# Attention rotation on GpSimd: eight 128x512 operations a step regrouped into four 128x1024 operations, with the minus sign moved into a VectorE product

## The reference

```python
def _apply_rope(x):
    ...
    x1, x2 = jnp.split(x, 2, axis=-1)
    rot = jnp.concatenate([-x2, x1], axis=-1)
    return x * cos + rot * sin
...
q = _apply_rope(proj(Wq, bq))        # 16 heads of 64
k = _apply_rope(proj(Wk, bk))
v = proj(Wv, bv)
scores = jnp.einsum('bhnqd,bhnkd->bhnqk', qb, kcat) * scale   # blocks of 128 queries, 256 keys
attn = jax.nn.softmax(jnp.where(valid, scores, -1e30), axis=-1)
ctx = jnp.einsum('bhnqk,bhnkd->bhnqd', attn, vcat)
return merged @ Wo.T + bo
```

## Time and profile before

| what | value |
|---|---|
| median of three runs | 1629.46 us (1627.92 to 1631.04) |
| span of the profiled execution, first to last instruction | 1627.8 us |
| own time of the profiled execution | not listed apart from the three runs |
| mean granted TensorE clock | 0.983 |
| VectorE busy from 300 to 1400 us | 999.38 us |
| TensorE busy from 300 to 1400 us | 1044.70 us |
| ScalarE busy from 300 to 1400 us | 905.92 us |
| GpSimd busy from 300 to 1400 us | 772.60 us |

### The profile page before, as it was taken

How to read it: one execution, slowest core, us unless ns; L and a number is a source line. 1 busy time by engine, 2 the same in 40 slices (tenths; PEclk the granted TensorE clock), 3 DMA queues, 4 the chain that set the end, 5 groups by cost and what they waited for, 6 DMA issues and landing times. The chain is left out here.

```text
span 1627.8 us, 46635 instructions
## 1 busy us (share of the span) xinstructions
PE 1505.6 (92%) x16930; PEld 1152.3 (71%) x16930; DVE 1401.5 (86%) x3881; ACT 1318.2 (81%) x2394; POOL 1031.1 (63%) x788
## 2 busy tenths in 40 slices
PE   5999978899999999999999999999999999869998
PEld 4888745576766777676767666766777677658887
DVE  5999678899999899999998998999899989857885
ACT  5999657888878888878887887878888878849996
POOL 4665267677667777767677776667777767513443
PEclk8999999999999999999999999999999999979999
DMA  5233246989998989899998999998989899962331
GB/s 210 91 124 107 78 85 120 175 152 191 157 184 162 179 157 181 168 176 176 163 179 157 179 164 175 157 182 163 175 162 182 154 174 154 176 159 69 109 106 75
DMA packets 721530, 247.90 MB, mean 152 GB/s; under 512 B 687380, under 2 KB 706072, under 8 KB 721304
## 3 DMA queue, kind: packets, MB, share of 16 engines
q1 hardware_dynamic: 720600, 244.53, 77.4%
q10 hardware_dynamic: 704, 0.40, 0.1%
HBM read 47.73 MB, written 25.17 MB: 45 GB/s over the span
## 5 line engine op out<-in xcount | busy, mean ns | idle before, releaser
L1450 ACT ACTIVATE at_prob<-at_prob,at_top 128x256 f32<-128x256 f32 (+1 forms) x1024 | 428.5, 490 | 42.1 <-DVE at_top L1262 39.0
L1262 DVE CUSTOM_DVE_ANT_0 at_prob<-banks,at_masks,pre_s_scale 128x256 f32<-128x256 f32 (+1 forms) x1024 | 420.3, 471 | 19.7 <-PE banks L1703 6.7
L1585 PE MATMUL banks<-at_xt,pre_w_h 128*128 128x512 f16 x1024 | 297.5, 383 | 22.6 <-ACT at_v_l L1478 21.9
L1274 DVE TENSOR_TENSOR at_halves<-at_prob,at_halves 128x1024 f16<-128x1024 f32 (+1 forms) x256 | 315.5, 1233 | 1.2 <-ACT at_halves L1459 1.2
L1703 PE MATMUL banks<-at_kt,at_qt 32*128 32x256 f32 (+1 forms) x4096 | 251.6, 382 | 38.8 <-POOL at_qt L1183 19.5
L1459 ACT ACTIVATE at_halves<-at_prob 128x1024 f16<-128x1024 f32 (+1 forms) x256 | 263.4, 1029 | 6.1
L1703 PEld LDWEIGHTS banks<-at_kt,at_qt 32*128 32x128 f32 x4096 | 197.4, 186 | 99.8 <-issue 95.5
L1204 POOL TENSOR_TENSOR at_c_halves<-at_ctx,at_c_halves 128x1024 f16<-128x1024 f32 x64 | 136.7, 2136 | 178.0 <-DVE at_halves L1274 172.4
L1173 POOL TENSOR_TENSOR at_kt<-at_k_by 128x512 f32<-128x512 f32 x128 | 163.2, 1275 | 95.6 <-DVE at_halves L1274 95.4
L1183 POOL TENSOR_TENSOR at_qt<-at_q_by 128x512 f32<-128x512 f32 x128 | 223.0, 1761 | 0.0
L1163 POOL TENSOR_TENSOR at_q_by<-at_q_first,at_tables 128x512 f32<-128x512 f32 x128 | 163.2, 1275 | 83.5 <-DVE at_halves L1274 83.5
(11 more groups left out here) (128 smaller groups left out, 3280.4 us busy)
## 6 DMA issues: line engine op xcount, KB each, us to landing
f_x<-in_x SPq DMA_DIRECT2D x16, 512.0 KB, 3.7
x_after_ffn<-f_x SPq DMA_DIRECT2D x16, 512.0 KB, 2.6
at_x_ln<-x_after_ffn SPq DMA_DIRECT2D x16, 512.0 KB, 3.5
at_x_res<-x_after_ffn SPq DMA_DIRECT2D x64, 128.0 KB, 3.0
x_after_attention<-at_x_res SPq DMA_DIRECT2D x64, 128.0 KB, 2.7
f_x<-x_after_attention SPq DMA_DIRECT2D x16, 512.0 KB, 4.6
out_x<-f_x SPq DMA_DIRECT2D x16, 512.0 KB, 3.0
at_tables<-in_cos SPq DMA_DIRECT2D x16, 256.0 KB, 4.0
```

What stands on the lines that cost most here:

```text
L1262: last = nc.vector.tensor_tensor_reduce(out=prob[:, n % 2, h, low:2 * P], in0=s_ps[:, h, n % 2 * 2 * P + low:(n % 2 + 1) * 2 * P], in1=mas ...
L1274: nc.vector.tensor_tensor(parts[:, 1, :, :], prob[:, n % 2, :, keys_from(t, b):2 * P], parts[:, 0, :, :], ALU.subtract).then_inc(p_low, 1)
L1450: last = nc.scalar.activation(at, at, ACT.Exp, bias=top[:, n % 2, h:h + 1], scale=-1.0)
L1585: last = nc.tensor.matmul(pr_ps[:, half, :].rearrange("p (b t) -> p b t", b=SB), w[wp][:, k, at:at + P], xt[:, r, xp, :, k, :], start=n == ...
```

## The change

The rotation is regrouped. On GpSimd the two products of a first half (with cos and with sin) become one operation of 128x1024, and so do the two halves of the sum. For this the difference becomes a sum: VectorE writes the sin product of the second half with its sign turned, as (-bias - x) sin, with a table of negated biases made once. Each step then has four GpSimd rotation operations where there were eight, and as many VectorE products as before. The semaphores of single products are merged: a consumer that waited for one half waits for both.

The order of the lists also differs. On GpSimd `key(t + 1)` (both halves) stands directly behind `after_p_low(t, 0)`, `query_products(t + 1)` behind it, and `query(t + 1)` behind `after_p_low(t, 1)`. On VectorE the two `query_product(t + 1)` stand together ahead of `context(t - 1, 1)`, `p_low_of(t, 2)` stands ahead of `shift_of`, and `p_low_of(t, 3)` ahead of `x_low_of`. On ScalarE `carry_keys` stands ahead of `query_copy`, and `key_copy(t + 2)` stands directly behind `v_low_of`, ahead of `normalize`, `x_high_of`, `p_high_of(t, 3)` and `context_high`.

```diff
@@ Prepared.vector
+            for n in range(2):
+                nc.vector.tensor_scalar(self.neg_bias[:, n, :], self.bias[:, n, :], w_up[:, n:n + 1], -1.0, ALU.mult,
+                                        ALU.mult)
@@ gpsimd
-                nc.gpsimd.tensor_tensor(k_by[:, n, :], k_first[:, :], tables[:, r, n // 3, :],
-                                        ALU.mult).then_inc(k_made[n], 1)
+                nc.gpsimd.tensor_tensor(k_by[:, 0:2, :], k_first[:, :].unsqueeze(1).broadcast_to([P, 2, SB * P]),
+                                        tables[:, r, :, :], ALU.mult).then_inc(k_first_made, 1)
...
+                nc.gpsimd.tensor_tensor(qt[:, t % 2, :, :], q_by[:, 0:2, :], q_by[:, 2:4, :],
+                                        ALU.add).then_inc(q_roped, 1)
@@ gpsimd at_step
             after_p_low(t - 1, 3)
             context_low(t - 2)
-            key_product(t + 1, 0)
-            key_product(t + 1, 3)
+            key_products(t + 1)
             after_p_low(t, 0)
-            key(t + 1, 1)
-            query_product(t + 1, 0)
+            key(t + 1)
+            query_products(t + 1)
             after_p_low(t, 1)
-            query_product(t + 1, 3)
+            query(t + 1)
             if g == 3 and S > -2:
                 inverse_std(S + 2)
-            key(t + 1, 0)
-            query(t + 1, 1)
-            query(t + 1, 0)
@@ vector, key_product and query_product alike
-                nc.vector.scalar_tensor_tensor(k_by[:, n, :], pr_ps[:, 1, :], bias[:, 1, 2 * g + 1:2 * g + 2],
-                                               tables[:, r, n % 2, :], ALU.add, ALU.mult).then_inc(k_made[n], 1)
+                by = (neg_bias, bias)[n][:, 1, 2 * g + 1:2 * g + 2]
+                nc.vector.scalar_tensor_tensor(k_by[:, 2 + n, :], pr_ps[:, 1, :], by, tables[:, r, 1 - n, :],
+                                               (ALU.subtract, ALU.add)[n], ALU.mult,
+                                               reverse0=n == 0).then_inc(k_second_made, 1)
@@ vector at_step
-            query_product(t + 1, 2)
+            query_product(t + 1, 0)
+            query_product(t + 1, 1)
             context(t - 1, 1)
-            query_product(t + 1, 1)
             p_low_of(t, 0)
...
+            p_low_of(t, 2)
             if g == 3 and S > -2:
                 shift_of(S + 2)
-            p_low_of(t, 2)
             residual(t - 5)
             context(t, 0)
+            key_product(t + 2, 0)
             key_product(t + 2, 1)
-            key_product(t + 2, 2)
+            p_low_of(t, 3)
             if g == 3 and S > -2:
                 x_low_of(S + 2)
-            p_low_of(t, 3)
@@ scalar at_step
             p_high_of(t, 0)
+            carry_keys(t - 1)
             query_copy(t + 1)
-            carry_keys(t - 1)
...
             v_low_of(t + 1, 1)
             v_low_of(t + 1, 0)
+            key_copy(t + 2)
             if g == 3 and S > -2:
                 normalize(S + 2)
-            if g == 3 and S > -2:
                 x_high_of(S + 2)
             p_high_of(t, 3)
             context_high(t - 1)
-            key_copy(t + 2)
```

More of the change, by code:

```diff
@@ L896, in attention_stage @@
     wo = (pre.wo_h, pre.wo_l)
-    bias = pre.bias
+    bias, neg_bias = pre.bias, pre.neg_bias
     ct = pre.raw[:, :, :].rearrange("p a b -> p (a b)").bitcast(F16).rearrange(
@@ L963, in attention_stage @@
     q_copied = sem("q_copied")
[L964 to L967, removed]
+    k_first_made = sem("k_first_made")
+    q_first_made = sem("q_first_made")
+    k_second_made = sem("k_second_made")
+    q_second_made = sem("q_second_made")
+    k_roped = sem("k_roped")
+    q_roped = sem("q_roped")
     k_carried = sem("k_carried")
@@ L1097, in load_tables @@
             if big(S):
-                for n in range(4):
-                    need(q_made[n], NG * (S - 1))
-                    need(k_made[n], NG * (S - 1))
+                for products, each in ((k_first_made, 1), (q_first_made, 1), (k_second_made, 2), (q_second_made, 2)):
+                    need(products, each * NG * (S - 1))
                 at = SB * P * (S % SPB)
@@ L1145, in gpsimd, with key_products @@
         need = Need(pool)
-        def key_product(t, n):
+        def key_products(t):
             if step(t):
@@ L1151, in key_product, with query_products @@
                 pool.wait_ge(k_copied, t + 1)
-                need(k_roped[n // 2], t)
-                nc.gpsimd.tensor_tensor(k_by[:, n, :], k_first[:, :], tables[:, r, n // 3, :],
-                                        ALU.mult).then_inc(k_made[n], 1)
-        def query_product(t, n):
+                need(k_roped, t)
+                nc.gpsimd.tensor_tensor(k_by[:, 0:2, :], k_first[:, :].unsqueeze(1).broadcast_to([P, 2, SB * P]),
+                                        tables[:, r, :, :], ALU.mult).then_inc(k_first_made, 1)
+        def query_products(t):
             if step(t):
@@ L1161, in query_product, with key, query @@
                 pool.wait_ge(q_copied, t + 1)
[L1162 to L1166, removed]
+                need(q_roped, t)
+                nc.gpsimd.tensor_tensor(q_by[:, 0:2, :], q_first[:, :].unsqueeze(1).broadcast_to([P, 2, SB * P]),
+                                        tables[:, r, :, :], ALU.mult).then_inc(q_first_made, 1)
+        def key(t):
             if step(t):
-                pool.wait_ge(k_made[2 * half], t + 1)
-                pool.wait_ge(k_made[2 * half + 1], t + 1)
+                pool.wait_ge(k_first_made, t + 1)
+                pool.wait_ge(k_second_made, 2 * t + 2)
                 need(s_done, 2 * t - 2)
                 need(k_carried, carried(t - 2))
[L1173 to L1177, removed]
+                nc.gpsimd.tensor_tensor(kt[:, :, own(t, 0):own(t, 0) + SB, :].rearrange("p h s t -> p h (s t)"),
+                                        k_by[:, 0:2, :], k_by[:, 2:4, :], ALU.add).then_inc(k_roped, 1)
+        def query(t):
             if step(t):
-                pool.wait_ge(q_made[2 * half], t + 1)
-                pool.wait_ge(q_made[2 * half + 1], t + 1)
+                pool.wait_ge(q_first_made, t + 1)
+                pool.wait_ge(q_second_made, 2 * t + 2)
                 need(s_done, 2 * t - 2)
-                nc.gpsimd.tensor_tensor(qt[:, t % 2, half, :], q_by[:, 2 * half, :], q_by[:, 2 * half + 1, :],
-                                        (ALU.subtract, ALU.add)[half]).then_inc(q_roped[half], 1)
+                nc.gpsimd.tensor_tensor(qt[:, t % 2, :, :], q_by[:, 0:2, :], q_by[:, 2:4, :],
+                                        ALU.add).then_inc(q_roped, 1)
         def inverse_std(S):
@@ L1344, in query_product @@
                 dve.wait_ge(q_done[1], t + 1)
-                need(q_roped[n // 2], t)
-                nc.vector.scalar_tensor_tensor(q_by[:, n, :], pr_ps[:, 1, :], bias[:, 0, 2 * g + 1:2 * g + 2],
-                                               tables[:, r, n % 2, :], ALU.add, ALU.mult).then_inc(q_made[n], 1)
+                need(q_roped, t)
+                by = (neg_bias, bias)[n][:, 0, 2 * g + 1:2 * g + 2]
+                nc.vector.scalar_tensor_tensor(q_by[:, 2 + n, :], pr_ps[:, 1, :], by, tables[:, r, 1 - n, :],
+                                               (ALU.subtract, ALU.add)[n], ALU.mult,
+                                               reverse0=n == 0).then_inc(q_second_made, 1)
         def first_moments():
@@ L1682, in scores @@
                 g, par = t % NG, t % 2
-                for half in range(2):
-                    pe.wait_ge(k_roped[half], t + 1)
-                    pe.wait_ge(q_roped[half], t + 1)
+                pe.wait_ge(k_roped, t + 1)
+                pe.wait_ge(q_roped, t + 1)
                 need(top_made, 4 * t + 2 * duo)
```

24 lines of the change are left out of this document (10 added, 14 removed).

## The result

The changed kernel takes 1976.12 us (median of 4 runs, 1972.84 to 1978.9) against 1628.69 us before. The ratio is 1.2132, 95% interval 1.2116 to 1.2149: slower by 347 us. The forecast was 1954 us in a range of 1895 to 2040. The profiled execution took 1978.9 us with a span of 1976.8 us.

A forecast was written before the change was run, and what follows sets the result against it. VectorE was taken to bound a step, closed by a short tail through ScalarE and TensorE. 290 + 23 - 5 + 16 = 324 us on 1627.8 gave 1952, forecast 1954 us with the median's 1.7 us; range 1895 to 2040.

The forecast's parts named there:

- order term: `key_copy` ahead of `p_high_of(t, 3)` on ScalarE delays `p_low_of(t, 3)`: 4.11 us a plain step, 6.62 with g = 3, 290 us.
- third rival: TensorE's clock falls in nearly every step, as a 3.1 us gap is enough: 68 us for the clock, 2005 us; chance 0.16.
- The conflicts at the port: GpSimd's larger operations meet `p_low_of(t, 1)`: 23 us lost in 14 steps with `moments`, 5 us won in the others.
- free collision of `p_low_of(t, 2)`: GpSimd's `query` collides with `p_low_of(t, 2)` at no cost while VectorE idles behind it; otherwise up to 2.2 us a step.
- second rival: A GpSimd operation of 2.14 us lets `query_products` hold off `p_low_of(t, 1)` in most steps: 102 us, total 2022 us; chance 0.20.
- The clock: TensorE idles longer and loses its full clock after g = 3 steps only: 15 to 17 us in all, bounds 0 and 68.
- Edits at nothing: Reversed subtraction, negated bias table, exchanged list neighbours and merged semaphores: taken at no cost, with small upper bounds.
- The far side: Faster: moving `key_copy` changes nothing and the stretch of two `p_low_of` goes away, 15 us, 1614 us; chance 0.02.
- g = 3 term: Part of the `key_copy` loss: 6.62 us in each of 14 steps with `normalize`, `x_low_of`'s 1.14 us included; 92.7 us.

The follow-up runs named there:

- gates_late_copy: The changed kernel with `key_copy` back at the end of ScalarE's step and GpSimd's `query_products` and `query` each gated one `p_low_of` later: 1641.5 us.
- filled_gates: The changed kernel with unread matmuls in TensorE's idle gap and GpSimd's `query_products` and `query` gated one `p_low_of` later, `key_copy` still early: 1899.25 us.
- gates_early_copy: The changed kernel with GpSimd's `query_products` behind `after_p_low(t, 1)` and `query` behind `after_p_low(t, 2)`, `key_copy` still early: 1929.36 us.
- copy_alone: The kernel before with one edit, `key_copy(t + 2)` moved directly behind `v_low_of` on ScalarE: 1926.84 us, ratio 1.1812.

## Why the prediction was right

**The sum.** From before to the changed kernel the runs make one path of single causes: the rest of the change +12.8 us (1628.69 to 1641.5, gates_late_copy), the place of `key_copy` with the clock held up +257.8 (to 1899.25, filled_gates), the clock +30.1 (to 1929.36, gates_early_copy), the conflicts at the port +46.8 (to 1976.12). They add up to 347.4 us by construction, and another order of the path gives other shares. With the copy late the same gates are worth 69 us (1710.6 to 1641.5), not 47. With the copy early the rest of the change costs not 12.8 but 2.5 us (copy_alone to gates_early_copy), and that is no more than noise, for gates_early_copy is known to some 8 us only. All steps but the second join runs that were measured beside different runs of the kernel before, whose medians differ by up to 3 us.

**How near, and why.** The forecast of 1954 us is 22 us short. Its terms were 290, 18 and 16 us; the path gives 271, 47 and 30. An order term that was 19 us too large covers part of 43 us that the two others lacked. So the mechanism of the main term is confirmed, and the closeness of the sum is in part luck. Of its signs, ScalarE's wait (4.6 us, forecast 5), VectorE's wait (4.1, forecast 4) and busy share (74%, forecast 72%), the 2.36 us of GpSimd and the g = 3 period (27.74, forecast 27) came. Two did not: `p_low_of(t, 1)` was long in 49 of 64 steps, and the g = 2 period was 24.02 us, not 22.5. The sign of the third rival came too, with a granted clock of 0.91 in the steady part where it asked for less than 0.93.

**The order of ScalarE's list**, forecast 290 us with the place of `x_low_of`: measured 258 us for the copy and at most 13 for all the rest, 271 us. The chain behind the copy was right to 0.04 us: from `key_copy` to `p_low_of(t, 3)` 1.66 us where I had 1.69, and 4.71 with `normalize` where I had 4.75. The stretch from `keys_of` to `key_copy` was oversized. I took 5.29 us as dense but for issue gaps and wrote that the GpSimd part can't shorten it. It does: `scores(t + 1, 0)` had been waiting for `query`, which ended at 805.82, 0.10 us before the scores started at 805.92. I had read this wait as an issue gap of TensorE. With the queries early the loop takes 5.55 us from `v_low` instead of 6.07. The bounds of 270 to 310 us for this term hold 271 and not 258, so they hold the value only if the whole rest is counted to it.

**The conflicts at the port**, forecast 23 - 5 us: 47 us measured, mis-sized by the number of steps. Duration (2.36 us), the winner of the race in undisturbed steps, and the loss with `moments` (1.6 us, measured 2.83 - 1.22) came out as worked out. What I didn't see is that a margin of 0.1 us falls in every step in which something else delays `p_low_of(t, 1)`: it exceeds 1.5 us in 49 of 64 steps of the changed kernel. The forecast's condition for the free collision of `p_low_of(t, 2)`, VectorE's idling behind it, held with the copy early. The second rival had this outcome with another mechanism, a shorter operation, and that one is out.

The Trainium skill, SBUF — State Buffer, section Who interferes with whom, has the second comer blocked until the first has finished, and the order of issue decide. The runs agree: `p_low_of(t, 1)` behind a `query_products` that is 0.6 us old takes 2.87 us, and 1.22 us in every step where the gates keep the two apart.

**The clock**, forecast 16 us from g = 3 steps alone: 30 us, and the third rival's mechanism was real: the clock fell behind gaps of 2.99 us too. Its price of 68 us was not. Clock and conflicts don't add up as separate terms, as I had them. The kernel takes 1976.12 us with neither taken away, 1929.36 without conflicts, 1911.26 without most of the low clock, and 1899.25 without both. Alone, the conflicts cost 12 us and the clock 30. Together they cost 77 us, for 35 us, known to some 8, are conflicts that only the low clock brings about.

The Trainium skill, TensorE: Matmul & The Clock Gate, Part 1, has the clock halved for an idle engine. The runs agree, with 3.17 to 3.79 us for scores that take 2.01 us at the full clock, and with 65 us won by matmuls that compute nothing of use.

**Edits at nothing.** The reversed subtraction costs next to nothing: 750 ns with the negated bias and 742 ns without, in the groups from 900 to 1100 us. GpSimd's smaller total is hidden, as forecast. Of the 11.6 us by which gates_late_copy's profiled span is longer than before, 5.7 lie ahead of the first `p_low_of(0, 3)` and 6.4 in steps 1 to 61; the place of `x_low_of`, which was part of the g = 3 term, fits the pattern of the steps and is not shown. **The far side** (faster) failed as argued: the copy never came early enough.

## What to carry to other kernels

A wait that costs nothing because it stands last in an engine's list costs nearly its whole length, each step, when it is moved ahead of work that another engine needs (in copy_alone a wait of 4.9 us on average, and 4.1 us more for a step with g = 2); price a reordering by what stands behind the wait, not by what the moved instruction takes. Two engines that share a port and are kept apart by a margin of 0.1 us are kept apart only as long as nothing shifts, so larger operations want one gate each. A longer loop opens gaps on TensorE, the gaps lower its clock, and the delay can push other work into conflicts: terms that are small one by one can cost more together than their sum (12 and 30 us alone, 77 us together).

## What the runs showed of the hardware

A GpSimd `tensor_tensor` of 128x1024 takes 2362 ns where all is float32, and 2136 ns where the output and the second input are float16; which of the two makes the difference is not shown. TensorE's granted clock was 0.58 in the 4 us behind a 2.99 us gap, and 1.00 in the 4 us that hold the gap itself. Filling the gap with unread matmuls took the kernel from 1976.12 to 1911.26 us.
